# Eight-bank attention loops in a fused four-layer decoder: whole sequences per turn instead of half sequences

## The chip, the core and the metric

The kernel runs on one NeuronCore of a Trainium2 chip. The metric is the device time of one execution in microseconds (us), as a median of several runs; lower is better. The engines that matter are TensorE (PE in the profile; PEld are its weight loads), VectorE (DVE), ScalarE (ACT) and GpSimd (POOL). PSUM, into which TensorE writes, has eight banks of 128 partitions by 512 fp32 values.

## What is computed

Twelve layers run one after the other on x of shape (8, 128, 128): eight sequences of 128 tokens with 128 features. Five of them are 16-head attentions with head size 8 (three self-attentions, L1a, L3a and, with keys and values from ctx, L0x, all causal; L1x with a distance bias; L2x with an integer mask). Each comes down to this (scaling, mask and projections differ):

```python
scores = jnp.einsum('bhqd,bhkd->bhqk', query, key_) * scale
scores = jnp.where(causal, scores, -jnp.inf)
probs = jax.nn.softmax(scores, axis=-1)
attn = jnp.einsum('bhqk,bhkd->bhqd', probs, value)
attn = attn.transpose(0, 2, 1, 3).reshape(Bq, Sq, D)
return attn @ Wo.T
```

So one sequence has 16 score matrices of 128x128, or 128x2048 fp32 values, which fill four PSUM banks. The other layers (gated experts, a linear attention, a router) are not touched by the change.

## The kernel before

All instructions are written by hand, engine by engine, with semaphores. The eight sequences are two groups (g = 0, 1) of four (GB = 4). Each engine has one program for each group; the programs are generators that yield a pair (layer, phase), and `weave` always continues the one with the smallest pair. So the order on an engine is fixed when the kernel is built, by the phases; inside an attention loop they come from `beat`.

One attention of one group is done in eight units (UNITS = 8), u = 2b + half: a unit is half of the heads (eight) of sequence b. Two row strips of 32 partitions hold these heads: strip r holds the four heads 4r to 4r+3, and `KTm` holds the keys spread so that a 32-row matmul gives four heads' scores in one bank. The steps of a unit, in the names that the text uses:

- **M** (`masked`, `biased`, PE): the mask or bias is written to the unit's two banks by bf16 matmuls with the identity; one per bank, three per bank in L1x.
- **S** (`scores`, PE): one 32-row fp32 matmul of 512 columns per strip is added to it, in a bank of its own. An fp32 matmul is two MATMUL records in the profile.
- **R** and **sub** (DVE, L1258 and L1264): the row maximum of each head over the unit's 1024 columns, then the scores minus the maximum, to SBUF (`pr`).
- **T** (`turned`, PE, L458): eight transposes back to the same two banks.
- **exp** (ACT, L892): the exponential of the two banks to SBUF (`PT`).
- **W** (`weighted`, PE): eight matmuls with 32 output columns each, the values with a column of ones, to the bank `VALUES[g]`.
- **OT** (`weighted_out`, ACT, L860): after both halves the 128x512 result is copied to SBUF.

After the last unit, **back** (PE, L477) transposes the four copies, DVE divides by the sum that the column of ones gave (`normal`, `normal_last`, L1231 to L1241), and `out_proj` and a residual add end the layer.

Banks 0 and 7 are `VALUES`. The other six are three pairs, which the units of both groups take in turn (`pair(g, u)` is `PAIRS[(2u + g) % 3]`), so M of a unit waits for the exp of an earlier unit of the other group. POOL (L347) spreads the keys of each sequence into one of two halves of `KTm`.

Of the kernel before, what the change touches and what calls it, by code (L numbers as in the profile page):

```python
# [11 lines left out]
ACT = mybir.ActivationFunctionType  # L12
AX = mybir.AxisListType

P = 128
# [76 lines left out]
def build(nc, x_d, ctx_d, mask_d, w_d, r_d, c_d, k_d, b_d, out_d, marks):  # L92
# [165 lines left out]
    def beat(g, u, k=0):  # L258

        return 20 + 10 * u + 6 * g + k  # L260
# [49 lines left out]
    def _(pool):  # L310
# [13 lines left out]
        def program(g):  # L324
# [7 lines left out]
            def spread_keys(n, l):  # L332

                first = 0 if l in ("L1x", "L2x") else 1
                for b in range(first, GB):
                    yield n, ((1 + b if first == 0 else 19) if b < 2 else beat(g, 2 * b - 4, 3))
                    if b == first:
                        pool.wait_ge(*s.at(f"{l}.KT"))
                        if l == "L0x":
                            for other in range(GROUPS):  # L340
                                pool.wait_ge(*s.at("L0x.qrot", other))
                        if first == 0:
                            for other in range(GROUPS):
                                pool.wait_ge(*s.at(f"{l}.xn", other))
                    if b >= 2:
                        pool.wait_ge(*s.at(f"{l}.S{2 * b - 3}"))
# [46 lines left out]
    def _(pe):  # L393
        def mm(out, lhsT, rhs, start=True, stop=True, **k):
            return pe.matmul(out, lhsT, rhs, start=start, stop=stop, **k)  # L395
# [5 lines left out]
        def program(g):  # L401
# [22 lines left out]
            def attend(n, l):  # L424

                def biased(u, i):

                    r, out = 2 * (u % 2) + i, pair(g, u)[:, i, :]
                    if l == "L1x":
                        odd = out.rearrange("p (j k) -> p j k", j=HG)[:, 1::2, :]  # L430
                        mm(out, identb, alibi0[:, HG * r:HG * r + HG, :], stop=False)
                        mm(odd, identb, alibi1[:, 2 * r:2 * r + 2, :], start=False, stop=False)
                        mm(odd, identb, alibi2[:, 2 * r:2 * r + 2, :], start=False, stop=False)
                    else:
                        mask = t.dmask[:, u // 2, :] if l == "L2x" else causalb
                        mm(out, identb, mask.unsqueeze(1).to_broadcast([P, HG, P]), stop=False)

                def masked(u):
                    if 2 * u + g >= 3:
                        pe.wait_ge(*s.at(f"{l}.exp{(2 * u + g - 3) // 2}", 1 - g))  # L440
                    elif u:
                        pe.wait_ge(*s.at(f"{l}.QT", 1))
                    for i in range(2):
                        biased(u, i)

                def scores(u):
                    b, half = divmod(u, 2)
                    if half == 0:
                        pe.wait_ge(*s.at(f"{l}.keys{b}"))
                    for i in range(2):  # L450
                        r = 32 * (2 * half + i)
                        ins = mm(pair(g, u)[:, i, :], QT[r:r + 32, b * P:(b + 1) * P], t.KTm[r:r + 32, b % 2, :, :], start=False, tile_position=(r, 0))
                    ins.then_inc(*s.step(f"S{u}"))

                def turned(u):
                    pe.wait_ge(*s.at(f"{l}.sub{u}"))
                    for j in range(HH):
                        ins = pe.transpose(heads_of(pair(g, u))[:, j // HG, j % HG, :], pr[:, (u % 2) * HH + j, :], ident)  # L458
                    ins.then_inc(*s.step(f"T{u}"))

                def weighted(u):

                    b, half = divmod(u, 2)
                    if half == 0 and b:
                        pe.wait_ge(*s.at(f"{l}.OT{b - 1}"))
                    pe.wait_ge(*s.at(f"{l}.exp{u}"))
                    for j in range(HH):
                        h, at = HH * half + j, 32 * (j % HG)
                        ins = mm(VALUES[g][at:at + 32, h // HG * P:(h // HG + 1) * P], t.vaug[:, b, h, :], PT[:, (u % 2) * HH + j, :], tile_position=(0, at))
                    ins.then_inc(*s.step(f"O{u}"))  # L470

                def back(b):

                    pe.wait_ge(*s.at(f"{l}.OT{b}"))
                    for i in range(GB):
                        out = (VALUES[g] if b == GB - 1 else EARLIER[g][:, b, :])[:, i * P:(i + 1) * P]
                        ins = pe.transpose(out, t.ot[b][:, i * P:(i + 1) * P], ident)  # L477
                    ins.then_inc(*s.step(f"OR{b}"))

                pe.wait_ge(*s.at(f"{l}.KT"))  # L480
                pe.wait_ge(*s.at(f"{l}.vaug"))
# [22 lines left out]
                yield n, beat(g, UNITS, 1)  # L504
                if g == 0:
                    pe.wait_ge(*s.at(f"{l}.exp{UNITS - 1}", 1))
                for b in range(GB - 1):
                    back(b)
                yield n, beat(g, UNITS, 2)
                back(GB - 1)  # L510
# [336 lines left out]
    def _(act):  # L847
# [5 lines left out]
        def program(g):  # L853
# [31 lines left out]
            def attend(n, l):  # L885
                for u in range(UNITS):
                    yield n, beat(g, u, 4)
# [3 lines left out]
                    half = PT[:, (u % 2) * HH:(u % 2 + 1) * HH, :].rearrange("p (i j) k -> p i j k", i=2)  # L891
                    act.activation(half, heads_of(pair(g, u)), ACT.Exp, scale=SCALES[l]).then_inc(*s.step(f"exp{u}"))  # L892
                    if u >= 2 and u % 2 == 0:
                        yield n, beat(g, u, 5)
                        weighted_out(u // 2 - 1, l)
                yield n, beat(g, UNITS, 1)
                weighted_out(GB - 1, l)
                yield n, 130
                read(t.coT[:, :], bank(3 * g), "coTp", "coT")

            def weighted_out(b, l):
                read(t.ot[b], VALUES[g], f"O{2 * b + 1}", f"OT{b}")

# [189 lines left out]
    def _(dve):  # L1093
# [50 lines left out]
        def program(g):  # L1144
# [82 lines left out]
            def attend(n, l):  # L1227
                def normal():
                    dve.wait_ge(*s.at(f"{l}.OR{GB - 2}"))
                    O = EARLIER[g].rearrange("p b (h d) -> p b h d", h=H)  # L1230
# [5 lines left out]
                def normal_last():  # L1236
                    dve.wait_ge(*s.at(f"{l}.OR{GB - 1}"))
                    O = VALUES[g].rearrange("p (h d) -> p h d", h=H)
# [14 lines left out]
                for u in range(UNITS):  # L1253
                    yield n, beat(g, u, 1)
                    half = u % 2
                    S, top = heads_of(pair(g, u)), t.mx[:, half, :].rearrange("p (i j) -> p i j", i=2)
                    dve.wait_ge(*s.at(f"{l}.S{u}"))
                    dve.tensor_reduce(top, S, AX.X, ALU.max).then_inc(*s.step())  # L1258
                    reduced = s.last()
                    yield n, beat(g, u, 2)  # L1260
                    if u >= 2:
                        dve.wait_ge(*s.at(f"{l}.T{u - 2}"))
                    dve.wait_ge(*reduced)
                    dve.tensor_tensor(pr[:, half * HH:(half + 1) * HH, :].rearrange("p (i j) k -> p i j k", i=2), S,  # L1264
                                      top.unsqueeze(3).to_broadcast([P, 2, HG, P]), ALU.subtract).then_inc(*s.step(f"sub{u}"))
                yield n, beat(g, UNITS, 2)
                normal()
                yield n, beat(g, UNITS, 3)
# [507 lines left out]
```

## Time and profile before

| what | us |
|---|---|
| median of 3 runs | 725.29 |
| lowest and highest | 724.2, 726.57 |
| the profiled execution's own time | 725.43 |
| span of its instructions | 723.6 |
| PE busy | 591.4 (82%) |
| DVE busy | 471.8 (65%) |
| ACT busy | 255.7 (35%) |
| POOL busy | 98.6 (14%) |

The span runs from the first to the last instruction on the core; the 1.8 us between it and the run's own time lie around it. A busy share is a mean over all twelve layers, which have different limits, so the attention loops are read by themselves. PE counts a matmul until its modelled end, and the next may start before that: starts of successive instructions tell more than their durations.

### The profile page before, as it was taken

How to read it: one execution, taken by the hardware profiler on the slowest of the kernel's cores; microseconds unless marked ns; L12 is line 12 of the kernel's file. 1: busy time of each engine (PE TensorE's matmuls, PEld its weight loads, DVE VectorE, ACT ScalarE, POOL GpSimd, SP SyncE). 2: the span in 40 equal slices, each digit the busy share in tenths (PEclk: the TensorE clock that was granted, in tenths of full speed). 3: DMA queues.
4: the chain of work that ended last, by engine and by line, in shares of the span. 5: the costliest groups of instructions: out<-in, count | busy, mean ns of one | idle time of the engine just before them, and what ended most of it. 6: DMA issues, size and time to landing. Idle time of an engine off the chain costs nothing.

```text
span 723.6 us, 10686 instructions
## 1 busy us (share of the span) xinstructions
PE 591.4 (82%) x4265; PEld 389.8 (54%) x4265; DVE 471.8 (65%) x1200; ACT 255.7 (35%) x380; POOL 98.6 (14%) x101
## 2 busy tenths in 40 slices
PE   1425699976999889988997788999779978998477
PEld 1324355676455645565776755556435574556435
DVE  7687777577587566755247726775553468866685
ACT  2356334414344333333432442434221114443261
POOL 5021120014210041001002004200200012102120
PEclk9967589979899999997998999999789989999769
DMA  9700000000000000000000000000000000000000
GB/s 293 327 0 2 0 1 2 1 1 1 0 2 1 1 1 1 2 1 1 0 1 1 1 0 1 1 2 1 0 1 0 1 1 0 2 1 1 0 1 29
DMA packets 6720, 12.40 MB, mean 17 GB/s; under 512 B 528, under 2 KB 4880, under 8 KB 6288
## 3 DMA queue, kind: packets, MB, share of 16 engines
q1 hardware_dynamic: 6672, 11.73, 4.5%
q8 instruction: 33, 0.54, 0.3%
q14 instruction: 15, 0.12, 0.1%
HBM read 11.21 MB, written 0.52 MB: 16 GB/s over the span
## 4 chain that ended last, share of the span: by engine, by line
PE 69%; DVE 23%; ACT 3%; POOL 3%; issue 2%; DVEq 0%; ACTq 0%; POOLq 0%
PE ps L395 52%; PE ps L458 11%; DVE st L1151 3%; PE ps L411 3%; PE ps L477 2%; DVE xn L1347 2%; DVE mx L1258 2%; DVE big L1264 2%; POOL rs L330 2%; DVE mv L1154 1%; DVE x L1277 1%; PE ps L580 1%; ACT big L892 1%; DVE big L1190 1%; DVE ve L1156 1%
## 5 line engine op out<-in xcount | busy, mean ns | idle before, releaser
L1258 DVE TENSOR_REDUCE mx<-ps 128x8 f32<-128x1024 f32 x80 | 97.9, 1224 | 53.1 <-PE ps L395 52.9
L892 ACT ACTIVATE big<-ps 128x1024 f32<-128x1024 f32 x80 | 81.9, 1023 | 125.5 <-PE ps L458 125.5
L1264 DVE TENSOR_TENSOR big<-ps,mx 128x1024 f32<-128x1024 f32 x80 | 98.0, 1225 | 7.3 <-DVE mx L1258 0.5
L458 PE MATMUL ps<-kt,big 128*128 128x128 f32 x640 | 90.1, 285 | 8.1 <-DVE big L1264 7.9
L395 PE MATMUL ps<-KTm,qk 32*128 32x512 f32 x320 | 92.7, 658 | 0.0
L458 PEld LDWEIGHTS ps<-kt,big 128*128 128x128 f32 x640 | 70.7, 144 | 34.6 <-DVE big L1264 19.7
L330 POOL TENSOR_TENSOR rs<-ve,negh 128x4 f32<-128x4 f32 x26 | 26.5, 1021 | 406.3 <-DVE ve L1156 406.2
L395 PE MATMUL ps<-xnT,wt 128*128 128x512 f32 (+1 forms) x140 | 73.8, 667 | 3.1 <-DVE big L1539 3.1
L395 PEld LDWEIGHTS ps<-wt,big 128*128 128x128 f32 (+1 forms) x480 | 56.0, 191 | 10.9 <-issue 8.6
L395 PE MATMUL ps<-wt,big 128*128 128x128 f32 (+1 forms) x480 | 60.2, 280 | 1.1 <-ACT big L1041 1.1
L395 PEld LDWEIGHTS ps<-big,vaug 128*32 128x32 f32 x1280 | 30.4, 109 | 48.0 <-ACT big L892 45.5
L347 POOL TENSOR_TENSOR KTm<-qk,kt 128x512 f32<-128x512 f32 x34 | 37.4, 1107 | 127.9 <-PE ps L395 88.0
L411 PE MATMUL ps<-kt,xn 128*128 128x128 f32 x80 | 18.8, 378 | 39.3 <-DVE xn L1347 39.0
L395 PE MATMUL ps<-big,vaug 128*32 128x128 f32 x1280 | 50.5, 278 | 0.0
L395 PE MATMUL ps<-bt 128*128 128x512 bf16 (+1 forms) x192 | 46.8, 354 | 0.0
L860 ACT ACTIVATE xnT<-ps 128x512 f32<-128x512 f32 x30 | 17.9, 597 | 75.8 <-PE ps L411 65.5
L395 PEld LDWEIGHTS ps<-xnT,wt 128*128 128x128 f32 (+1 forms) x140 | 27.6, 212 | 31.6 <-issue 26.0
L395 PEld LDWEIGHTS ps<-KTm,qk 32*128 32x128 f32 x320 | 24.8, 189 | 33.9 <-issue 31.3
L1323 DVE SCALAR_TENSOR_TENSOR x<-ps,gw,x 128x128 f32<-128x128 f32 x80 | 22.2, 344 | 30.3 <-PE ps L395 29.5
L395 PEld LDWEIGHTS ps<-wt,xnT 128*128 128x128 f32 x256 | 38.1, 237 | 3.4 <-DVE big L1495 1.7
L395 PE MATMUL ps<-wt,xnT 128*128 128x128 f32 (+2 forms) x256 | 38.4, 313 | 1.5 <-DVE big L1495 1.5
L411 PEld LDWEIGHTS ps<-kt,xn 128*128 128x128 f32 x80 | 12.0, 187 | 44.4 <-issue 25.9
(274 smaller groups left out, 773.4 us busy)
## 6 DMA issues: line engine op xcount, KB each, us to landing
wt<-in_weights SPq DMA_DIRECT2D x1, 1664.0 KB, 17.3
wt<-in_weights SPq DMA_DIRECT2D x1, 1603.0 KB, 12.3
wt<-in_weights SPq DMA_DIRECT2D x6, 256.0 KB, 11.3
bt<-in_bconsts SPq DMA_DIRECT2D x1, 1024.0 KB, 8.7
rowt<-in_rows SPq DMA_DIRECT2D x1, 975.0 KB, 5.7
wt<-in_weights SPq DMA_DIRECT2D x1, 832.0 KB, 13.8
wt<-in_weights SPq DMA_DIRECT2D x1, 608.0 KB, 18.5
wt<-in_weights SPq DMA_DIRECT2D x1, 580.0 KB, 5.5
```

What stands on the lines that cost most here:

```text
L330: pool.tensor_tensor(out, src, negh[:, :], ALU.pow).then_inc(*s.step(name + "_r"))
L347: pool.tensor_tensor(t.KTm[:, b % 2, :, :], keys_of(t, b), own_head(), ALU.mult).then_inc(*s.step(f"keys{b}"))
L395: return pe.matmul(out, lhsT, rhs, start=start, stop=stop, **k)
L411: ins = pe.transpose(seq(bk, b), src[:, b, :], ident)
L458: ins = pe.transpose(heads_of(pair(g, u))[:, j // HG, j % HG, :], pr[:, (u % 2) * HH + j, :], ident)
L477: ins = pe.transpose(out, t.ot[b][:, i * P:(i + 1) * P], ident)
L860: act.activation(out, src, ACT.Copy).then_inc(*s.step(name))
L892: act.activation(half, heads_of(pair(g, u)), ACT.Exp, scale=SCALES[l]).then_inc(*s.step(f"exp{u}"))
L1151: dve.bn_stats(t.st[:, b, :], src[:, b, :]).then_inc(*s.step())
L1258: dve.tensor_reduce(top, S, AX.X, ALU.max).then_inc(*s.step())
L1264: dve.tensor_tensor(pr[:, half * HH:(half + 1) * HH, :].rearrange("p (i j) k -> p i j k", i=2), S, top.unsqueeze(3).to_broadcast([P, 2, HG ...
L1323: dve.scalar_tensor_tensor(x[:, b, :], bank(banks[e])[:, b * P:(b + 1) * P], gw[:, b, e:e + 1], x[:, b, :], ALU.mult, ALU.add).then_inc(*s ...
```

## The change

The two groups no longer share banks. Group g has banks 4g to 4g+3, and all four hold the scores of one whole sequence: strip r in bank r.

- M is written for four banks and S runs all four strips in a row, once for each sequence, with one semaphore step; `scores(b)` was two calls of two strips.
- R, sub, T, exp and W stay as they were in size and number (eight heads each). They work on `pair(g, half)`, banks 0 and 1 or 2 and 3 of the group.
- W of half 0 goes to bank 0 and W of half 1 to bank 2, each to 256 columns, after the exp of that half has read them. Each is copied by an own OT of 128x256. The masks of the next sequence follow bank by bank: bank 1 and bank 3 after the W, bank 0 and bank 2 after their OT.
- `back` writes sequence b to bank (b+1) % 4 of the group, in the order 0, 2, 1, 3.
- The phases (`beat`) count turns: turn 2b + g is sequence b of group g.

```diff
-    PAIRS = (all_banks[:, 1:3, :], all_banks[:, 5:7, :], all_banks[:, 3:5, :])
-    EARLIER = (all_banks[:, 1:4, :], all_banks[:, 4:7, :])
-    VALUES = tuple(all_banks[:, k, :] for k in (0, 7))
-
-    def pair(g, u):
-
-        return PAIRS[(2 * u + g) % 3]
+    def pair(g, half):
+
+        return all_banks[:, 4 * g + 2 * half:4 * g + 2 * half + 2, :]
...
-                def scores(u):
-                    b, half = divmod(u, 2)
-                    if half == 0:
-                        pe.wait_ge(*s.at(f"{l}.keys{b}"))
-                    for i in range(2):
-                        r = 32 * (2 * half + i)
-                        ins = mm(pair(g, u)[:, i, :], QT[r:r + 32, b * P:(b + 1) * P], t.KTm[r:r + 32, b % 2, :, :], start=False, tile_position=(r, 0))
-                    ins.then_inc(*s.step(f"S{u}"))
+                def scores(b):
+                    pe.wait_ge(*s.at(f"{l}.keys{b}"))
+                    for i in range(GB):
+                        r = 32 * i
+                        ins = mm(bank(i), QT[r:r + 32, b * P:(b + 1) * P], t.KTm[r:r + 32, b % 2, :, :], start=False, tile_position=(r, 0))
+                    ins.then_inc(*s.step(f"S{b}"))
...
-                masked(0)
+                masked(0, 1)
+                pe.wait_ge(*s.at(f"{l}.vaug"))
+                masked(0, 2)
                 if l in ("L1x", "L2x"):
                     yield n, 4
                     pe.wait_ge(*s.at(f"{l}.xnT"))
                     project_cols(0, xnT, w(f"{l}_wq"), "q")
+                masked(0, 3)
                 yield n, 20
                 pe.wait_ge(*s.at(f"{l}.QT"))
+                masked(0, 0)
                 scores(0)
-                for u in range(UNITS):
-                    yield n, beat(g, u, 2)
-                    turned(u)
-                    if u + 1 < UNITS:
-                        masked(u + 1)
-                        scores(u + 1)
-                    if u:
-                        weighted(u - 1)
-                yield n, beat(g, UNITS)
-                weighted(UNITS - 1)
...
+                for b in range(GB):
+                    turn, more = 2 * b + g, b + 1 < GB
+                    yield n, beat(turn - 1, 5)
+                    turned(2 * b)
+                    yield n, beat(turn, 0)
+                    turned(2 * b + 1)
+                    weighted(2 * b)
+                    if more:
+                        masked(b + 1, 1)
+                    weighted(2 * b + 1)
+                    if more:
+                        masked(b + 1, 3)
+                        pe.wait_ge(*s.at(f"{l}.OT{2 * b}"))
+                        masked(b + 1, 0)
+                        yield n, beat(turn, 6)
+                        pe.wait_ge(*s.at(f"{l}.OT{2 * b + 1}"))
+                        masked(b + 1, 2)
+                        scores(b + 1)
```

On PE, in the middle of the loop of L0x, the rows before are these, for one unit of each group (kt,big is T, bt is M, KTm,qk is S, big,vaug is W; the digit is the group; L395 and L391 are the helper that issues every matmul):

```order
L458 MATMUL ps<-kt,big0 128x128 x8
L395 MATMUL ps<-bt 128x512 x2
L395 MATMUL ps<-KTm0,qk0 128x512 x2
L395 MATMUL ps<-big0,vaug0 32x128 x8
L458 MATMUL ps<-kt,big1 128x128 x8
L395 MATMUL ps<-bt 128x512 x2
L395 MATMUL ps<-KTm1,qk1 128x512 x2
L395 MATMUL ps<-big1,vaug1 32x128 x8
```

And now, for one turn (one sequence of group 0) from its second T to its S:

```order
L444 MATMUL ps<-kt,big0 128x128 x8
L391 MATMUL ps<-big0,vaug0 32x128 x8
L391 MATMUL ps<-bt 128x512
L391 MATMUL ps<-big0,vaug0 32x128 x8
L391 MATMUL ps<-bt 128x512 x2
L444 MATMUL ps<-kt,big1 128x128 x8
L391 MATMUL ps<-bt 128x512
L391 MATMUL ps<-KTm0,qk0 128x512 x4
```

The W of a unit stood behind the S of the next one; now both W of a sequence stand between its second T and its next S, with the masks in between and the first T of the other group before the last mask.

On ACT, in the same place, before (L892 is exp, L860 is OT):

```order
L892 ACTIVATE big0<-ps 128x1024
L860 ACTIVATE td0<-ps 128x512
L892 ACTIVATE big1<-ps 128x1024
L860 ACTIVATE td1<-ps 128x512
L892 ACTIVATE big0<-ps 128x1024
```

And now:

```order
L884 ACTIVATE big0<-ps 128x1024 x2
L853 ACTIVATE td0<-ps 128x256 x2
L884 ACTIVATE big1<-ps 128x1024 x2
L853 ACTIVATE td1<-ps 128x256 x2
L884 ACTIVATE big0<-ps 128x1024 x2
```

The copies come right behind the second exp of their own sequence, where one copy for each sequence stood behind the first exp of the next.

## Rows read from the trace of the kernel before

**Rows 1.** The page, part 1: busy time, share and instructions of each engine.

```profile
PE 591.4 (82%) x4265; PEld 389.8 (54%) x4265; DVE 471.8 (65%) x1200; ACT 255.7 (35%) x380; POOL 98.6 (14%) x101
```

**Rows 2.** The page, part 5, the S matmuls: count | busy us, mean ns.

```profile
L395 PE MATMUL ps<-KTm,qk 32*128 32x512 f32 x320 | 92.7, 658 | 0.0
```

**Rows 3.** Windows from first R to last sub, per loop: engines' busy us, PEclk.

```profile
83.71:134.48 50.77, 50.34 (x418) 26.80 (x417) 39.20 (x32) 18.88 (x21) 4.16 (x4) 0.89 0.00 1
...
191.99:238.85 46.86, 45.35 (x418) 24.52 (x416) 39.10 (x32) 18.89 (x21) 4.16 (x4) 1.00 0.00 1
260.36:313.18 52.82, 50.66 (x472) 29.69 (x468) 39.10 (x32) 18.89 (x21) 5.04 (x5) 1.00 0.00 1
447.57:495.73 48.16, 45.92 (x416) 25.06 (x412) 39.10 (x32) 18.89 (x21) 5.75 (x6) 0.96 0.00 1
602.00:648.85 46.85, 45.35 (x418) 24.52 (x416) 39.10 (x32) 19.29 (x22) 4.88 (x5) 1.00 0.00 1
```

**Rows 4.** Timeline in the loop of L0x: start, us, engine, line, tiles, count.

```profile
107.23 1.22 DVE L1258 TENSOR_REDUCE mx<-ps 128x8 f32<-128x1024 f32 x1 [0.53 <-PE ps L395]
...
107.69 1.09 PE L458 MATMUL ps<-kt,big 128*128 128x128 f32 x8
...
108.56 1.23 DVE L1264 TENSOR_TENSOR big<-ps,mx 128x1024 f32<-128x1024 f32 x1
108.61 0.60 PE L395 MATMUL ps<-bt 128*128 128x512 bf16 x2
108.81 1.02 ACT L892 ACTIVATE big<-ps 128x1024 f32<-128x1024 f32 x1 [0.40 <-PE ps L458]
...
109.14 1.13 PE L395 MATMUL ps<-KTm,qk 32*128 32x512 f32 x4
...
110.20 0.64 PE L395 MATMUL ps<-big,vaug 128*32 128x128 f32 x16
110.31 1.23 DVE L1258 TENSOR_REDUCE mx<-ps 128x8 f32<-128x1024 f32 x1 [0.53 <-PE ps L395]
...
110.77 1.09 PE L458 MATMUL ps<-kt,big 128*128 128x128 f32 x8
```

**Rows 5.** Timeline at the end of the loop of L0x.

```profile
134.53 1.09 PE L458 MATMUL ps<-kt,big 128*128 128x128 f32 x8 [0.49 <-DVE big L1264]
...
135.55 1.08 PE L395 MATMUL ps<-big,vaug 128*32 128x128 f32 x32
135.66 1.02 ACT L892 ACTIVATE big<-ps 128x1024 f32<-128x1024 f32 x1 [1.13 <-PE ps L458]
...
136.74 0.66 PE L477 MATMUL ps<-kt,td 128*128 128x128 f32 x4
```

**Rows 6.** Timeline at the starts of the loops of L1a and L1x.

```profile
190.29 0.59 PE L395 MATMUL ps<-bt 128*128 128x512 bf16 x2
...
190.81 0.30 PEld L395 LDWEIGHTS ps<-KTm,qk 32*128 32x128 f32 x4 [0.42 <-issue]
...
257.38 1.88 PE L395 MATMUL ps<-xnT,wt 128*128 128x512 f32 x4
...
259.19 1.99 PE L395 MATMUL ps<-KTm,qk 32*128 32x512 f32 x8
...
263.83 1.03 PE L395 MATMUL ps<-bt 128*128 128x512 bf16 x6
```

**Rows 7.** Windows as in Rows 3, at the starts of L0x and L2x.

```profile
74.00:94.50 20.50, 15.89 (x46) 7.48 (x48) 13.66 (x16) 5.54 (x8) 3.92 (x3) 0.50 0.00 0
...
449.50:452.90 3.40, 2.79 (x12) 1.89 (x12) 2.91 (x3) 0.79 (x1) 0.00 (x0) 0.50 0.00 0
```

**Rows 8.** Timeline in these stretches: T in L2x, M and S in L0x.

```profile
450.11 1.97 PE L458 MATMUL ps<-kt,big 128*128 128x128 f32 x8 [1.73 <-DVE big L1264]
...
80.60 1.06 PE L395 MATMUL ps<-bt 128*128 128x512 bf16 x2
...
81.59 2.08 PE L395 MATMUL ps<-KTm,qk 32*128 32x512 f32 x4
```

More of the change, by code:

```diff
@@ L256, in last, with beat @@
             return semaphores[self.sem], self.count[self.sem] - back
-    def beat(g, u, k=0):
-        return 20 + 10 * u + 6 * g + k
+    def beat(turn, k=0):
+        return 30 + 10 * turn + k
     SCALES = {l: float(P if l == "L2x" else HD) ** -0.5 for l in ("L0x", "L1a", "L1x", "L2x", "L3a")}
@@ L335, in spread_keys @@
                 for b in range(first, GB):
-                    yield n, ((1 + b if first == 0 else 19) if b < 2 else beat(g, 2 * b - 4, 3))
+                    yield n, ((1 + b if first == 0 else 19) if b < 2 else beat(2 * (b - 2) + g))
                     if b == first:
@@ L345, in spread_keys @@
                     if b >= 2:
-                        pool.wait_ge(*s.at(f"{l}.S{2 * b - 3}"))
+                        pool.wait_ge(*s.at(f"{l}.S{b - 2}"))
                     pool.tensor_tensor(t.KTm[:, b % 2, :, :], keys_of(t, b), own_head(), ALU.mult).then_inc(*s.step(f"keys{b}"))
@@ L424, in attend, with masked @@
             def attend(n, l):
-                def biased(u, i):
-                    r, out = 2 * (u % 2) + i, pair(g, u)[:, i, :]
+                def masked(b, r):
+                    out = bank(r)
                     if l == "L1x":
@@ L434, in biased @@
                     else:
-                        mask = t.dmask[:, u // 2, :] if l == "L2x" else causalb
+                        mask = t.dmask[:, b, :] if l == "L2x" else causalb
                         mm(out, identb, mask.unsqueeze(1).to_broadcast([P, HG, P]), stop=False)
[L438 to L442, printed above, removed]
-                    for i in range(2):
-                        biased(u, i)
-                def scores(u):
-                    b, half = divmod(u, 2)
-                    if half == 0:
-                        pe.wait_ge(*s.at(f"{l}.keys{b}"))
-                    for i in range(2):
-                        r = 32 * (2 * half + i)
-                        ins = mm(pair(g, u)[:, i, :], QT[r:r + 32, b * P:(b + 1) * P], t.KTm[r:r + 32, b % 2, :, :], start=False, tile_position=(r, 0))
-                    ins.then_inc(*s.step(f"S{u}"))
+                def scores(b):
[4 more added lines that the diff above has]
+                    ins.then_inc(*s.step(f"S{b}"))
                 def turned(u):
@@ L457, in turned @@
                     for j in range(HH):
[L458 removed]
+                        ins = pe.transpose(heads_of(pair(g, u % 2))[:, j // HG, j % HG, :], pr[:, (u % 2) * HH + j, :], ident)
                     ins.then_inc(*s.step(f"T{u}"))
@@ L463, in weighted @@
                     b, half = divmod(u, 2)
-                    if half == 0 and b:
-                        pe.wait_ge(*s.at(f"{l}.OT{b - 1}"))
                     pe.wait_ge(*s.at(f"{l}.exp{u}"))
                     for j in range(HH):
-                        h, at = HH * half + j, 32 * (j % HG)
-                        ins = mm(VALUES[g][at:at + 32, h // HG * P:(h // HG + 1) * P], t.vaug[:, b, h, :], PT[:, (u % 2) * HH + j, :], tile_position=(0, at))
+                        at = 32 * (j % HG)
+                        ins = mm(bank(2 * half)[at:at + 32, j // HG * P:(j // HG + 1) * P], t.vaug[:, b, HH * half + j, :], PT[:, half * HH + j, :],
+                                 tile_position=(0, at))
                     ins.then_inc(*s.step(f"O{u}"))
                 def back(b):
-                    pe.wait_ge(*s.at(f"{l}.OT{b}"))
                     for i in range(GB):
-                        out = (VALUES[g] if b == GB - 1 else EARLIER[g][:, b, :])[:, i * P:(i + 1) * P]
-                        ins = pe.transpose(out, t.ot[b][:, i * P:(i + 1) * P], ident)
+                        ins = pe.transpose(seq((b + 1) % GB, i), t.ot[b][:, i * P:(i + 1) * P], ident)
                     ins.then_inc(*s.step(f"OR{b}"))
                 pe.wait_ge(*s.at(f"{l}.KT"))
-                pe.wait_ge(*s.at(f"{l}.vaug"))
                 if l == "L1x":
@@ L490, in attend @@
                     project_cols(0, xnT, w(f"{l}_wq"), "q")
+                masked(0, 3)
                 yield n, 20
                 pe.wait_ge(*s.at(f"{l}.QT"))
+                masked(0, 0)
                 scores(0)
-                for u in range(UNITS):
-                    yield n, beat(g, u, 2)
-                    turned(u)
-                    if u + 1 < UNITS:
-                        masked(u + 1)
-                        scores(u + 1)
-                    if u:
-                        weighted(u - 1)
-                yield n, beat(g, UNITS)
-                weighted(UNITS - 1)
[L504 to L509, printed above, removed]
+                for b in range(GB):
[16 more added lines that the diff above has]
+                        scores(b + 1)
+                yield n, beat(2 * GB + g)
+                back(0)
+                back(2)
+                pe.wait_ge(*s.at(f"{l}.OT{UNITS - 1}"))
+                back(1)
                 back(GB - 1)
@@ L885, in attend, with exponentials @@
             def attend(n, l):
-                for u in range(UNITS):
-                    yield n, beat(g, u, 4)
+                def exponentials(u):
+                    half = u % 2
                     act.wait_ge(*s.at(f"{l}.T{u}"))
@@ L890, in attend, with weighted_out @@
                         act.wait_ge(*s.at(f"{l}.O{u - 2}"))
[L891 to L897, printed above, removed]
+                    act.activation(PT[:, half * HH:(half + 1) * HH, :].rearrange("p (i j) k -> p i j k", i=2), heads_of(pair(g, half)),
+                                   ACT.Exp, scale=SCALES[l]).then_inc(*s.step(f"exp{u}"))
+                def weighted_out(u):
+                    b, half = divmod(u, 2)
+                    read(t.ot[b][:, 2 * half * P:2 * (half + 1) * P], bank(2 * half)[:, 0:2 * P], f"O{u}", f"OT{u}")
+                for b in range(GB):
+                    turn = 2 * b + g
+                    yield n, beat(turn - 1, 5)
+                    exponentials(2 * b)
+                    yield n, beat(turn, 0)
+                    exponentials(2 * b + 1)
+                    weighted_out(2 * b)
+                    weighted_out(2 * b + 1)
                 yield n, 130
                 read(t.coT[:, :], bank(3 * g), "coTp", "coT")
-            def weighted_out(b, l):
-                read(t.ot[b], VALUES[g], f"O{2 * b + 1}", f"OT{b}")
             for n, l in enumerate(LAYERS[1:STAGES + 1]):
@@ L1228, in normal @@
                 def normal():
-                    dve.wait_ge(*s.at(f"{l}.OR{GB - 2}"))
-                    O = EARLIER[g].rearrange("p b (h d) -> p b h d", h=H)
+                    dve.wait_ge(*s.at(f"{l}.OR1"))
+                    O = all_banks[:, 4 * g + 1:4 * g + GB, :].rearrange("p b (h d) -> p b h d", h=H)
                     dve.reciprocal(t.rc3[:, :, :], O[:, :, :, HD]).then_inc(*s.step())
@@ L1237, in normal_last @@
                     dve.wait_ge(*s.at(f"{l}.OR{GB - 1}"))
-                    O = VALUES[g].rearrange("p (h d) -> p h d", h=H)
+                    O = bank(0).rearrange("p (h d) -> p h d", h=H)
                     dve.reciprocal(t.rc[:, :], O[:, :, HD]).then_inc(*s.step())
@@ L1253, in attend @@
                 for u in range(UNITS):
[L1254 to L1257, printed above, removed]
+                    b, half = divmod(u, 2)
+                    yield n, beat(2 * b + g, 1 + half)
+                    S, top = heads_of(pair(g, half)), t.mx[:, half, :].rearrange("p (i j) -> p i j", i=2)
+                    dve.wait_ge(*s.at(f"{l}.S{b}"))
                     dve.tensor_reduce(top, S, AX.X, ALU.max).then_inc(*s.step())
-                    reduced = s.last()
-                    yield n, beat(g, u, 2)
                     if u >= 2:
                         dve.wait_ge(*s.at(f"{l}.T{u - 2}"))
-                    dve.wait_ge(*reduced)
+                    dve.wait_ge(*s.last())
                     dve.tensor_tensor(pr[:, half * HH:(half + 1) * HH, :].rearrange("p (i j) k -> p i j k", i=2), S,
                                       top.unsqueeze(3).to_broadcast([P, 2, HG, P]), ALU.subtract).then_inc(*s.step(f"sub{u}"))
-                yield n, beat(g, UNITS, 2)
+                yield n, beat(2 * GB + g, 2)
                 normal()
-                yield n, beat(g, UNITS, 3)
+                yield n, beat(2 * GB + g, 3)
                 normal_last()
```

## The prediction, before the changed kernel ran

> **What bounds the kernel now.** I read the page's busy shares first: PE 82%, DVE 65% [rows 1]. These are means over twelve layers, so next the windows of the five attention loops, cut from the first R to the last sub. In all of them PE is busy nearly throughout: 45.35 of 46.86 us in L1a, 50.66 of 52.82 in L1x, while DVE has 39.1 in each [rows 3]. Together the loops last 245.5 us, a third of the run, and nothing outside them is changed except their starts and ends. The timeline of one unit in L0x then gives the cycle [rows 4]. T starts at 107.69, M at 108.61, S at 109.14, W at 110.20, the next T at 110.77: T 0.92, M 0.53, S 1.06, W 0.57, in sum 3.08 us with no gap. R starts at 107.23 and again at 110.31, the same 3.08. DVE works 2.46 of it and waits 0.53 for PE. So PE sets the pace, at 6.17 us for the two units of a sequence.
>
> **What S costs, and why it can shrink.** Two strips take 1.06 us from start to start of what follows. The four S records of a unit have a mean of 658 ns (92.7 us of PE for 320 of them [rows 2]), yet four fit in 1.13 us [rows 4]: the two strips run side by side and the two passes of fp32 one behind the other. The W of a unit, sixteen records of four column strips, fit in 0.64 us [rows 4], so four strips of the other kind run side by side already. Four row strips, each with its own bank, don't stand in the trace. From below, nothing is added for strips 2 and 3 (S stays 1.06 for a whole sequence); from above, they run behind the first two (2.12). I take 1.06, because both W and the pairs of S show full overlap; the upper end is a rival below. By this PE has 1.06 less work for each sequence, 5.1 instead of 6.17.
>
> The Trainium skill weighs here (TensorE: Matmul & The Clock Gate, part 3, measured speedup against the span model): its model adds some 4 ns per strip, as I take it, but its table gives four row strips of 512 columns as 3.07 times one, not 4. The trace agrees with the model for two strips (four records in 1.13 us). The table is the second rival.
>
> **One turn, step by step** (start = second T of group 0's sequence; PE order as in the order of the changed kernel). T to W is 1.02 (134.53 to 135.55 [rows 5]), since the kind of matmul changes. First W 0.57, to 1.59. One M, about half of 0.53, to 1.9. The second W needs the second exp. That one starts 1.13 after its T starts, takes 1.02, and lets PE go on 2.21 after T (134.53, 135.66, 136.74 [rows 5]). So the second W starts at 2.21, and PE has stood for 0.3: a new wait, with W, three M, the other group's T and S queued behind it. W to 2.78, M of banks 3 and 0 to 3.31, T of the other group 0.92 to 4.23 (its sub ended long before, see below), M of bank 2 0.27 to 4.50, S 1.06 to 5.56. The two OT waits add nothing: a copy of 256 columns is bounded by 1.02 us, the 1024-column exp, and I estimate 0.4; the first starts at 2.15 behind the exp and is done by 2.6, before 3.05 when M of bank 0 comes; the second starts at 2.85 and is done by 3.3, before 4.23. ACT is busy some 2.9 of 5.55. POOL's spread of the keys waits for the S of two sequences before, which is done two turns earlier, and POOL is busy 4 to 6 us in a whole loop [rows 3]. **A turn takes 5.55 us against 6.17.**
>
> DVE per sequence: R to sub 1.33 (107.23 to 108.56), sub 1.23, twice, in sum 5.15 [rows 4]. That is under 5.55, so PE stays the bound by 0.4, and the gain of 1.06 on PE loses 0.3 to the exp wait and some 0.1 to changes of kind.
>
> **A whole loop is not 8 turns.** Before, the first units run faster than 3.08, as there is no W yet: 46.86 us in L1a, not 16 x 3.08 = 49.3. Now the start is DVE's: first R at 0, last sub of group 0 at 5.15, T at 5.20. Turns 0 to 5 each issue the S for two turns later, whose R starts 1.17 after S (109.14 to 110.31), 5.67 after the turn's start. The last sequence's R starts at 5.20 + 5 x 5.55 + 5.67 = 38.6, its last sub ends at **43.8 us**. In L1x a mask has three matmuls; six for two banks last about 1.0 us where two last 0.53 [rows 6, 4], so 0.22 more per bank; one is hidden under the exp wait, three are not: turn 6.2, loop 5.20 + 31.0 + 6.3 + 5.15 = 47.7.
>
> **Starts.** Group 0 now needs four banks masked before its first S. In L1a and L3a PE is the bound there (M at 190.29, S at 190.81, no gap [rows 6]): +0.5 each. In L2x and L1x M of bank 3 of both groups moves behind the projections and M of bank 0 behind QT: three masks between the projection and S, less the slack until QT is ready: about +0.65 in L2x, 3 x 0.48 = +1.4 in L1x (projections from 257.38, S at 259.19 [rows 6]). In L0x the clock is at half and two masks cost 1.06 of PE [rows 8]: +0.9.
>
> **Ends.** After the last sub: T, W, exp wait, W, now 16 `back` transposes of each group without a W between them, where one W stood between. By the same steps it comes out within 0.2 us of before: nothing.
>
> **Sum against the profiled execution's own time, 725.4** (0.1 above the median). L1a and L3a: 46.86 to 43.8, less 0.5, saves 2.5 each. L2x: 48.16 to 43.8, less 0.65, saves 3.7. L1x: 52.82 to 47.7, less 1.4, saves 3.7. L0x starts at half clock until 94.5 [rows 7]: first R at 84.6, T of turn 0 only at 90.2, W, M and W at half speed, S at 96.4, then 5.55 a turn: last sub at 130.5 against 134.48, saves 4.0. Total 16.4, which gives 709.0.
>
> **The clock takes some back.** The granted clock was 0.50, that is 1.2 of 2.4 GHz, from 449.50 to 452.90, at the start of L2x's loop [rows 7]; PE had just stood for 1.73 us waiting for the first sub, and T took 1.97 instead of 1.09 [rows 8]. Now PE stands longer at every start: in the first 5.2 us it has S of group 1 and a single T, some 2 us of waiting. I assume that in three of the four starts that were at full clock the clock falls once for some 3.4 us, at 1 us each: T is 0.9 longer and partly on the path. That is +3 us. **Forecast 712.0 us, 13.4 less.** It could be 0 (709) or, with longer falls, +8 (717).
>
> **Rivals.**
> 1. *Four strips overlap only in part.* By 4/3.07 a set of four would take 1.30 times one strip's time, S 1.38 instead of 1.06: +0.32 in six places of each of five loops and in the first S, 35 times, +11 us: 723. For it: writing four banks at once is new. Against it: two row strips and four column strips show no loss at all. The factor is the table's of the skill page named above; any loss of 0.3 would give the same.
> 2. *The strips don't overlap by more than two.* S is 2.12, a turn 6.6, a plain loop 50.0 (5.20 + 33.0 + 6.7 + 5.15), the first S 1.06 later: L1a and L3a +4.7 each, L2x and L1x about +3.5 each, L0x +4, in sum +20: **745, slower**. It decides from an S of about 1.5 on, where 35 times the excess is the 16.4 us saved above. Then the exp wait, the later starts and the lost fast first units are paid without a gain.
> 3. *DVE is the bound.* If the changes of kind cost less and the exp wait closes, a turn falls to DVE's 5.15: 0.4 x 6 x 5 = 12 us less; that needs PE to find work for the wait, which its order doesn't allow. Half of it is thinkable: 705.
> 4. *Nothing changes*, since starts and the clock eat it all: each loop would have to lose 3.3 us more than above. The clock would have to be at half for most of turn 0 and 1 in all loops: about 722 to 727.
>
> **Chances.** Forecast with its clock term between 0 and +6 (708 to 716): 0.58. Rival 3 or part of it: 0.12. Rival 1 or more clock loss (716 to 723): 0.17. Rival 4: 0.06. Rival 2 or another slower case: 0.07. The range 704 to 722 leaves out about 0.17. A measurement tells about 0.3% from no change (2.2 us): faster 0.89, same 0.04, slower 0.07.
>
> **What the profile after would show.** The eight S records of a sequence within about 1.15 us, their starts in two sets of four (rival 2: four sets of two, 2.2 us; rival 1: records longer than 692 ns). R of successive sequences every 5.55 us, with DVE idle about 0.4 before the first R and none before the second. PE idle about 0.3 before the second W, released by exp. Loops near 44 us, 48 in L1x. PE's busy time lower by some 40 us, DVE's and POOL's unchanged, ACT's up by some 7 (40 more copies, half as long). A granted clock of 0.5 in the first 10 us of loops that had 1.0. I would be wrong if S is longer with four banks written at once, if PE waits for an OT, or if the first turns lose more than 1 us each to the clock.

## The result

The changed kernel takes **699.59 us** (median of 4 runs, 699.31 to 701.01); before, 724.75 (median of 4 runs, 723.8 to 726.57). The ratio is 0.9654, 95% interval 0.963 to 0.9678. That is 25 us less, where 13.4 were forecast, and below the range of 704 to 722. The direction and the overlap of four strips came as predicted; what the prediction said of the clock did not, and the forecast of 712.0 is 12.4 us above the median.

The page after, parts 1 and 5, stands against [rows 1, 2]:

```profile
PE 546.0 (78%) x4265; PEld 374.0 (54%) x4265; DVE 467.8 (67%) x1200; ACT 258.2 (37%) x420; POOL 98.6 (14%) x101
...
L391 PE MATMUL ps<-KTm,qk 32*128 32x512 f32 x320 | 46.5, 652 | 0.0
```

PE is busy 45 us less, and the 320 S records account for all of it: 92.7 to 46.5 us at the same mean of one (658 and 652 ns). They overlap by four where they overlapped by two.

The windows of the five loops after (first R to last sub, columns as in [rows 3]), then of the stretch behind L3a's loop, after and before:

```profile
84.79:127.76 42.97, 37.96 (x428) 22.62 (x426) 38.35 (x32) 19.96 (x29) 4.17 (x4) 1.00 0.00 1
185.74:228.72 42.98, 37.98 (x428) 22.62 (x426) 38.35 (x32) 19.96 (x29) 4.17 (x4) 1.00 0.01 1
251.27:298.52 47.25, 42.84 (x475) 26.56 (x473) 38.34 (x32) 19.96 (x29) 4.17 (x4) 1.00 0.01 1
433.18:476.15 42.97, 37.32 (x425) 22.44 (x424) 38.34 (x32) 19.96 (x29) 5.23 (x6) 1.00 0.00 1
582.32:625.30 42.98, 37.98 (x428) 22.64 (x426) 38.35 (x32) 19.96 (x29) 4.38 (x5) 1.00 0.01 1
625.30:697.50 72.20, 51.00 (x302) 35.21 (x302) 46.64 (x218) 24.54 (x43) 10.48 (x10) 0.89 0.03 8
...
648.85:723.60 74.75, 53.99 (x318) 37.50 (x318) 46.65 (x218) 25.13 (x44) 10.48 (x10) 0.86 0.03 8
```

All four plain loops take the same time, with the clock at full speed in all of them. L0x gains 7.8 us, L1a and L3a 3.9, L1x 5.6, L2x 5.2: 26.3 in sum. Of this some 5 us are clock: before, L0x's loop is 3.9 and L2x's 1.3 us longer than L1a's, each with a stretch at a granted 0.50 at its start [rows 3, 7], and now all are equal. The starts give back some 2.8; the stretch behind the last loop, whose work nobody changed, is 2.6 shorter here.

One turn of L0x after (timeline; T is L444, S has KTm,qk, W has big,vaug, M has bt):

```profile
100.68 1.09 PE L444 MATMUL ps<-kt,big 128*128 128x128 f32 x8
100.82 1.22 DVE L1256 TENSOR_REDUCE mx<-ps 128x8 f32<-128x1024 f32 x1 [0.47 <-PE ps L391]
...
101.70 0.64 PE L391 MATMUL ps<-big,vaug 128*32 128x128 f32 x16
...
102.28 0.39 PE L391 MATMUL ps<-bt 128*128 128x512 bf16 x1
...
102.89 0.64 PE L391 MATMUL ps<-big,vaug 128*32 128x128 f32 x16 [0.22 <-ACT big L884]
103.28 1.21 DVE L1256 TENSOR_REDUCE mx<-ps 128x8 f32<-128x1024 f32 x1
103.46 0.61 PE L391 MATMUL ps<-bt 128*128 128x512 bf16 x2
...
103.91 1.04 PE L444 MATMUL ps<-kt,big 128*128 128x128 f32 x8
...
104.78 0.38 PE L391 MATMUL ps<-bt 128*128 128x512 bf16 x1
...
105.09 1.14 PE L391 MATMUL ps<-KTm,qk 32*128 32x512 f32 x8
106.16 1.09 PE L444 MATMUL ps<-kt,big 128*128 128x128 f32 x8
```

Eight S records fit in 1.14 us, where four took 1.13 [rows 4], and the next T follows 1.07 after S, where it was 1.06. A turn is 5.48 us (100.68 to 106.16). DVE waits 0.47 for PE before the first R of a sequence and not before the second; PE waits 0.22 for exp (L884) before the second W. The prediction had 5.55, 0.4 and 0.3.

### The profile page after: what moved, and what is told of

Its sections match the earlier page's. It is cut to its first block, busy times and chain, and to the rows that moved or that the text cites. A ratio compares the mean times of both kernels' runs of the same rounds, so it can differ in the third digit from the quotient of the medians.

```text
span 697.5 us, 10675 instructions
## 1 busy us (share of the span) xinstructions
PE 546.0 (78%) x4265; PEld 374.0 (54%) x4265; DVE 467.8 (67%) x1200; ACT 258.2 (37%) x420; POOL 98.6 (14%) x101
## 4 chain that ended last, share of the span: by engine, by line
PE 63%; DVE 23%; ACT 8%; POOL 2%; issue 2%; DMA 1%; SPq 0%; DVEq 0%; ACTq 0%
PE ps L391 46%; PE ps L444 10%; ACT big L884 5%; PE ps L407 3%; DVE st L1149 3%; DVE big L1260 3%; PE ps L460 2%; DVE mx L1256 2%; DVE xn L1343 2%; POOL rs L326 2%; DMA co<-in_ctx 1%; DVE mv L1152 1%; DVE x L1273 1%; PE ps L573 1%; DVE ve L1154 1%
## 5 line engine op out<-in xcount | busy, mean ns | idle before, releaser
L884 ACT ACTIVATE big<-ps 128x1024 f32<-128x1024 f32 x80 | 81.9, 1023 | 114.8 <-PE ps L444 114.8
L444 PE MATMUL ps<-kt,big 128*128 128x128 f32 x640 | 85.7, 277 | 17.3 <-DVE big L1260 17.3
L444 PEld LDWEIGHTS ps<-kt,big 128*128 128x128 f32 x640 | 70.7, 141 | 52.4 <-DVE big L1260 43.1
L391 PE MATMUL ps<-xnT,wt 128*128 128x512 f32 (+1 forms) x140 | 74.6, 670 | 3.1 <-DVE big L1535 3.1
L391 PEld LDWEIGHTS ps<-wt,big 128*128 128x128 f32 (+1 forms) x480 | 56.0, 191 | 10.3 <-issue 8.6
L391 PE MATMUL ps<-wt,big 128*128 128x128 f32 (+1 forms) x480 | 60.1, 279 | 0.8 <-ACT big L1039 0.8
L391 PE MATMUL ps<-big,vaug 128*32 128x128 f32 x1280 | 51.5, 279 | 10.6 <-ACT big L884 10.6
L391 PE MATMUL ps<-bt 128*128 128x512 bf16 (+1 forms) x192 | 49.4, 352 | 0.0
L391 PE MATMUL ps<-KTm,qk 32*128 32x512 f32 x320 | 46.5, 652 | 0.0
L853 ACT ACTIVATE xnT<-ps 128x512 f32<-128x512 f32 (+1 forms) x40 | 19.6, 489 | 70.3 <-PE ps L407 65.5
L391 PEld LDWEIGHTS ps<-big,vaug 128*32 128x32 f32 x1280 | 30.1, 109 | 28.8 <-ACT big L884 22.1
L391 PEld LDWEIGHTS ps<-xnT,wt 128*128 128x128 f32 (+1 forms) x140 | 27.7, 214 | 31.1 <-issue 25.6
L391 PEld LDWEIGHTS ps<-wt,xnT 128*128 128x128 f32 x256 | 38.3, 238 | 3.4 <-DVE big L1491 1.7
L391 PE MATMUL ps<-wt,xnT 128*128 128x128 f32 (+2 forms) x256 | 38.4, 313 | 1.5 <-DVE big L1491 1.5
L1535 DVE TENSOR_TENSOR big<-ps,big 128x512 f32<-128x512 f32 (+1 forms) x18 | 12.3, 689 | 29.1 <-PE ps L391 29.1
```

The source lines that it names most:

```text
L444: ins = pe.transpose(heads_of(pair(g, u % 2))[:, j // HG, j % HG, :], pr[:, (u % 2) * HH + j, :], ident)
L853: act.activation(out, src, ACT.Copy).then_inc(*s.step(name))
L884: act.activation(PT[:, half * HH:(half + 1) * HH, :].rearrange("p (i j) k -> p i j k", i=2), heads_of(pair(g, half)), ACT.Exp, scale=SCALE ...
```

## Experiments: is the gain the overlap of four strips?

**s_pairs: the order undone that lets four strips stand in a row.** The mask of bank 2 moves between strips 1 and 2, from the second sequence of each group on; all instructions stay.

```diff
                     for i in range(GB):
                         r = 32 * i
+                        if b and i == 2:
+                            pe.wait_ge(*s.at(f"{l}.OT{2 * b - 1}"))
+                            masked(b, 2)
...
-                        pe.wait_ge(*s.at(f"{l}.OT{2 * b + 1}"))
-                        masked(b + 1, 2)
                         scores(b + 1)
```

> The changed kernel with one order undone: from the second sequence on, the mask of bank 2 stands between strips 0, 1 and strips 2, 3 of S, so that only two strips can run side by side; the instructions are the same. Theory 1 (the gain is that strips 2 and 3 cost nothing beside 0 and 1): S takes two times 1.06 and a turn goes from 5.48 to about 6.6; 5 loops x 6 turns x 1.1 = +33 us, 733 us, slower than before. Theory 2 (the gain comes from the new order and the own banks, S being of little weight): under +10 us, below 710.

Measured: 733.71 us, ratio to before 1.0118 (1.0093 to 1.0144), so 1.2% slower than before, a small difference that is clear of the noise. Its timeline in L1a:

```profile
208.43 1.13 PE L391 MATMUL ps<-KTm,qk 32*128 32x512 f32 x4
209.49 0.39 PE L391 MATMUL ps<-bt 128*128 128x512 bf16 x1
209.81 1.13 PE L391 MATMUL ps<-KTm,qk 32*128 32x512 f32 x4
210.87 1.09 PE L447 MATMUL ps<-kt,big 128*128 128x128 f32 x8
```

From S to the next T it is 2.44 us now (208.43 to 210.87), with the mask in it. Theory 1 expected 733. New order, own banks and split W by themselves make the kernel 9 us slower; the four strips side by side are worth 34 us, more than the whole gain. This is the prediction's second rival in all but the first S of each group, which keeps its four strips here. The rival had 745, 11 us more: about 5 (five times 1.06) for those first S, some 3 for L0x at half clock until 94.5 (here the clock is up at 84.6, as in the changed kernel), and 2.6 for the stretch behind the last loop. Its plain loop of 50.0 us measured 49.84.

**two_strips: strips 2 and 3 left out.**

```diff
-                    for i in range(GB):
+                    for i in range(2):
                         r = 32 * i
...
```

In banks 2 and 3 the mask matmuls' `start` and `stop` flags change with it, as no S is added there; their number and order stay.

> The changed kernel without the S of strips 2 and 3 (half of the scores is left out; everything else, masks, exponentials and W of all heads too, stays). Theory 1 (strips 2 and 3 run beside 0 and 1 and cost nothing): the turn stays at 5.48 to within 0.03, 699 to 700 us. Theory 2 (four banks written at once cost something, the skill table's 3.07 for 4): S falls by up to 0.3, up to 9 us faster.

Measured: 699.41 us, ratio 0.9641 (0.9583 to 0.97). Its timeline shows a turn of 5.47 us and four S records in 1.13:

```profile
100.46 1.13 PE L391 MATMUL ps<-KTm,qk 32*128 32x512 f32 x4
101.52 1.09 PE L444 MATMUL ps<-kt,big 128*128 128x128 f32 x8
...
105.93 1.13 PE L391 MATMUL ps<-KTm,qk 32*128 32x512 f32 x4
```

Two strips cost 1.06 us on PE and four 1.07. The prediction's first rival, an S of 1.38, is out. (This is the rival of the table; the sentence of the prediction that calls the table the second rival has the number wrong.) The two totals agree partly by chance, since in two_strips the clock was low in the first turns of L0x and L2x. Where it was at 1.00 in both kernels the loops can be compared: 42.85 us with two strips and 42.98 with four in L1a, 47.13 and 47.25 in L1x.

The Trainium skill (TensorE: Matmul & The Clock Gate, part 3, measured speedup against the span model) has a speedup of 3.07 for four row strips of 512 columns in its table, and some 4 ns for each further strip in its span model. By the table the prediction estimated 1.38 us. This trace is near the model and not the table: two further strips add 0.01 us.

## Experiments: what sets the turn now?

**exp_halves: the second exponential in two instructions.** The first half starts after four of the eight transposes.

```diff
+                        if u % 2 and j == HG - 1:
+                            ins.then_inc(*s.step(f"T{u}a"))
...
+                    if half:
+                        act.wait_ge(*s.at(f"{l}.T{u}a"))
+                        if u >= 2:
+                            act.wait_ge(*s.at(f"{l}.O{u - 2}"))
+                        for i in range(2):
+                            if i:
+                                act.wait_ge(*s.at(f"{l}.T{u}"))
+                            act.activation(PT[:, HH + i * HG:HH + (i + 1) * HG, :], heads_of(pair(g, 1))[:, i], ACT.Exp,
+                                           scale=SCALES[l]).then_inc(*s.step(f"exp{u}"))
+                        return
```

> The changed kernel with the second exponential of each sequence in two instructions of 512 columns, the first started after four of the eight transposes, so that the second W need not wait. Theory 1 (the wait of about 0.25 us for that exp is on the path, as PE sets the turn): a turn goes from 5.48 to about 5.25 in the plain loops, unchanged in L1x to within 0.05; 4 x 6 x 0.23 + ends = -5 to -6 us, 694 us. Theory 2 (DVE, which works 5.03 of 5.48, or the longer ACT time takes over): less than 2 us gained.

Measured: 693.05 us, ratio 0.9558 (0.9536 to 0.9581), 6.5 us less than the changed kernel. A turn of 5.19 us in its timeline:

```profile
100.37 1.09 PE L444 MATMUL ps<-kt,big 128*128 128x128 f32 x8
100.49 1.23 DVE L1268 TENSOR_REDUCE mx<-ps 128x8 f32<-128x1024 f32 x1 [0.18 <-PE ps L391]
...
102.29 0.64 PE L391 MATMUL ps<-big,vaug 128*32 128x128 f32 x16
...
105.56 1.09 PE L444 MATMUL ps<-kt,big 128*128 128x128 f32 x8
```

The second W starts 1.92 us after T instead of 2.21, and PE no longer stands before it. The exp wait that the change brought was on the path: 0.29 us of each plain turn. L1x gained a little too, against the expectation: its loop took 46.82 us instead of 47.25.

**grouped: besides, the mask of bank 1 before the first W**, so that both W stand together:

```diff
                     turned(2 * b + 1)
-                    weighted(2 * b)
                     if more:
+                        pe.wait_ge(*s.at(f"{l}.exp{2 * b}"))
                         masked(b + 1, 1)
+                    weighted(2 * b)
                     weighted(2 * b + 1)
```

> The kernel with the halved second exponential, and besides the mask of bank 1 moved from between the two W to before the first, so that both W stand together and PE changes its kind of matmul two times less in a turn. Theory 1 (a change of kind costs PE some 0.09 each and PE still sets the turn of 5.19): the turn goes to about 5.0, where DVE (4.91 busy and its gaps) takes over; 0.15 x 30 = -4 to -5 us against 693.05, 688.5 us. Theory 2 (a wait for the second half of the exp takes the place of what is saved, or DVE is the bound already): within 1 us of 693.

Measured: **685.79 us**, ratio 0.9449 (0.939 to 0.9507), the fastest kernel here and faster than both given ones. Its timeline:

```profile
99.88 1.09 PE L444 MATMUL ps<-kt,big 128*128 128x128 f32 x8
99.92 1.22 DVE L1269 TENSOR_REDUCE mx<-ps 128x8 f32<-128x1024 f32 x1
...
101.12 1.24 PE L391 MATMUL ps<-big,vaug 128*32 128x128 f32 x32
...
104.99 1.09 PE L444 MATMUL ps<-kt,big 128*128 128x128 f32 x8
105.12 1.23 DVE L1269 TENSOR_REDUCE mx<-ps 128x8 f32<-128x1024 f32 x1 [0.20 <-PE ps L391]
```

A turn is 5.11 (99.88 to 104.99) and the next one 5.2, where about 5.0 was expected, and DVE waits at every second sequence only. The median is 7.3 us below exp_halves, where 4 to 5 were expected. The loops of the two profiled executions hold 4.4 of it: L1x went from 46.82 to 45.35 us (bias matmuls stood between its two W), three plain loops from 41.26 to 40.90, and L2x from 42.75 to 40.90, as the clock had fallen in its start in exp_halves. Of the 1.9 us in L2x, 1.5 are therefore the clock's and not the edit's. The rest, some 3 us, lies outside the loops, in work that is the same in both, 2.1 of it behind the last loop (75.5 and 73.4 us); I put it down to the clock of the two executions, which wasn't separated. In L1x a turn went from 6.06 to 5.82 us, 0.12 for each change of kind that is gone. A plain turn gains less, as waits take the place of what is saved: the two W start 1.17 us before the next mask there (101.12 to 102.29) and 1.01 in L1x.

## Experiments: where does the clock come in?

The loop of L0x gained 7.8 us, twice as much as L1a's; 3.9 of it are clock. In before it starts at a granted clock of 0.50 until 94.5 us [rows 7]; in the changed kernel this ends at 84.6:

```profile
71.00:84.60 13.60, 6.90 (x24) 3.24 (x24) 8.85 (x15) 6.64 (x10) 2.88 (x2) 0.50 0.00 0
84.60:94.50 9.90, 7.80 (x80) 4.61 (x80) 9.52 (x8) 3.19 (x5) 2.08 (x2) 1.00 0.01 2
```

Is that the kernel or the execution? Both kernels were profiled again.

**b_again**, the kernel before:

> The kernel before, unchanged, profiled once more. Question: is its slow start of L0x's loop (granted clock 0.50 until 94.5 us, loop 50.77 us) and of L2x's loop (0.50 from 449.5 to 452.9, loop 48.16) a property of the kernel or of one execution? Theory A (property: the first units of before give TensorE too little work at these places): L0x's loop again 50 to 51 us, L2x's above 47.5. Theory B (chance of an execution): these two loops scatter, L0x's between 47 and 51, and other loops may be the slow ones. Both expect 723 to 727 us.

**a_again**, the changed kernel:

> The changed kernel, unchanged, profiled once more. Theory A: all four plain loops again 42.97 us and L1x 47.25, with the clock at 1.00 in all of them. Theory B: one or more loops show a stretch at 0.50 and are 1 to 3 us longer. The stretch after L3a's loop (72.20 us here, 74.75 in before) should be the same under A, and scatter by 1 to 3 us under B. Both expect 699 to 701 us.

726.51 and 701.29 us. Before: L0x's loop 50.91 us (clock low until 95.6), L2x's 48.16, L1a's 46.85: the same to 0.2 us. After: L0x's 42.95 (low until 87.3), but in L1a the clock fell once, for one stretch, and that loop took 44.21 instead of 42.98. Windows of L1a in a_again, loop and stretch:

```profile
188.11:232.32 44.21, 39.43 (x428) 23.57 (x426) 38.36 (x32) 20.09 (x29) 4.16 (x4) 0.96 0.01 1
...
193.10:196.50 3.40, 3.40 (x28) 2.22 (x28) 3.37 (x3) 1.41 (x2) 0.00 (x0) 0.50 0.00 0
```

So a fall of the clock in the first turns costs 1.2 us, near the prediction's 1 us, but it is rare: in the three profiled executions of the changed kernel (a third is below) the twelve starts other than L0x's show it once, where I had assumed three in four. Of the variants, exp_halves and two_strips show one each, in L2x, at 1.5 and 1.9 us. The stretch behind L3a's loop was 74.2 us, 2 longer than in the first profile, so its 2.6 us of gain can't be credited to the change. For the kernel before Theory A holds at both places: L2x's loop is 48.16 us in all three of its profiled executions (b_fourth is below), with the same stretch of 3.4 us at 0.50. For the changed kernel it holds in L0x's loop, and Theory B at the one fall in L1a and in the stretch behind L3a.

**first_pairs: only the first S of each group in two pairs.**

```diff
                     for i in range(GB):
                         r = 32 * i
+                        if b == 0 and i == 2:
+                            masked(0, 2)
...
-                masked(0, 2)
```

> The changed kernel with the first S of each group in two pairs, the mask of bank 2 between them; the later S as four strips. Looks at the granted clock at the start of L0x's loop, which left 0.50 at 84.6 and 87.3 us in two executions of the changed kernel and only at 94.5 and 95.6 in two of before. Theory A (four strips side by side in the first S are what brings the clock up): it stays at 0.50 into the nineties, and L0x's loop is 2 us or more longer than 43. Theory B (not S but the doubled masks or the moment decide): up by about 88, loop at 43 to 44. Both expect first R some 1 us later in each loop, about 5 us in all.

Measured: 706.96 us. The clock in L0x stayed low to 95.6 and its loop took 46.0 us; L1a's loop was 42.95, as in the changed kernel. Windows of first_pairs, to be held against those of the changed kernel above:

```profile
84.60:94.50 9.90, 9.90 (x25) 3.46 (x25) 6.22 (x6) 0.00 (x0) 2.08 (x2) 0.50 0.00 0
...
87.11:133.12 46.01, 42.89 (x428) 24.70 (x427) 38.43 (x32) 19.98 (x29) 4.16 (x4) 0.91 0.00 1
191.67:234.62 42.95, 39.07 (x428) 22.92 (x426) 38.33 (x32) 19.98 (x29) 4.16 (x4) 1.00 0.01 1
```

The total is 7.4 us above the changed kernel, 5 of it expected from the later starts. One execution could be chance, so first_pairs and both given kernels were profiled once more, as first_pairs_3, a_fourth and b_fourth.

> The kernel whose first S of each group is in two pairs, profiled a second time. So far the clock at the start of L0x's loop came up at 91.1 us or later in all four executions whose first S has two strips at a time (before twice, this kernel once, the one without strips 2 and 3 once) and by 87.3 in all five whose first S has four. Theory A (four strips at once bring it up): again after 90, L0x's loop 44 to 46 us. Theory B (chance of the execution): as likely by 88 with a loop near 43.

> The changed kernel, profiled once more. Theory A: the clock is up by 88 us and L0x's loop takes 42.97 us. Theory B: it may stay low into the nineties, with a loop of 44 to 46.

> The kernel before, profiled once more. Theory A: the clock stays low past 91 us, L0x's loop 48 to 51 us. Theory B: it may be up by 88, with a loop near 47.

Theory A three times: clock low until 98.1, 83.2 and 95.4; loops of L0x 46.81, 42.95 and 50.85 us (712.24, 697.98 and 723.86 us in all). The same window in a_fourth, b_fourth and first_pairs_3:

```profile
83.20:95.40 12.20, 10.12 (x104) 5.75 (x104) 10.68 (x9) 3.90 (x6) 3.12 (x3) 1.00 0.00 1
...
83.20:95.40 12.20, 12.20 (x36) 5.35 (x34) 7.35 (x6) 2.05 (x2) 1.61 (x2) 0.50 0.00 0
...
83.20:95.40 12.20, 12.20 (x32) 4.39 (x29) 7.04 (x6) 0.38 (x1) 2.44 (x3) 0.50 0.00 0
```

Counted over all runs: with two strips at a time in the first S the clock came up at 91.1 or later in six of six executions (before three times, first_pairs twice, two_strips once), with four at a time by 87.3 in six of six (the changed kernel three times, s_pairs, exp_halves, grouped). That the first S decides rests on two kernels: first_pairs differs from the changed kernel in the pairs of the first S and the place of one mask, and two_strips leaves all masks where they are and halves S (its later S too, and it ran in one profiled execution). So neither the doubled masks nor the place of that mask alone explains it. PE had no gap while the clock stayed low: 9.90 of 9.90 us in first_pairs, 12.20 of 12.20 in b_fourth. Why it stays low with two strips at a time is not settled: the runs show only that the same S records, side by side by four, go with an early rise in every execution.

## Why the prediction was wrong in size

Held against its own steps, from 712.0 down to the profiled 699.3:

| step | predicted | measured | adds |
|---|---|---|---|
| clock falls at the other loops' starts | +3 | 0 in this execution | 3.0 |
| L0x at half clock until 94.5, as before | loop 45.9, of which 43.8 at full clock | full clock | 2.1 |
| length of a loop at full clock, five loops | 43.8, 47.7 | 42.97, 47.25 | 3.8 |
| starts of the loops | +4.0 | +2.8 | 1.2 |
| stretch behind the last loop | 0 | -2.6 | 2.6 |

- **The clock was the step that failed**, with 5.1 of the 12.7 us. "The clock takes some back" had the price about right and the number of falls wrong: three in four starts assumed, none in this execution, one in twelve over three. It argued from PE's waiting. PE did wait 1.86 of the first 5.20 us of L1a's loop, near the 2 us predicted, and the clock stayed at 1.00, while the PE of L0x's start, busy without a gap, stayed at 0.50 in before. I had carried before's clock in L0x over as if it were given; it went with the two-strip S that the change removes. The 2.6 us behind the last loop are scatter that no step could have forecast: that stretch took 72.2 to 74.8 us over the executions of both kernels.
- **The loop's length** was the other term that was too large, with 3.8 us: the first sequence takes DVE 4.88 us to the end of its last sub (the next R starts at 4.79), not 5.15, since its sub has no wait for a T (R to sub 1.26 us instead of 1.33); the last takes 5.03; and the turn is 5.48, not 5.55. Three small sums on the high side, 0.8 us in each plain loop. Rows on DVE in L1a of the changed kernel:

```profile
185.74 1.23 DVE L1256 TENSOR_REDUCE mx<-ps 128x8 f32<-128x1024 f32 x1 [1.53 <-PE ps L391]
187.00 1.22 DVE L1260 TENSOR_TENSOR big<-ps,mx 128x1024 f32<-128x1024 f32 x1
188.15 1.21 DVE L1256 TENSOR_REDUCE mx<-ps 128x8 f32<-128x1024 f32 x1
...
190.53 1.22 DVE L1256 TENSOR_REDUCE mx<-ps 128x8 f32<-128x1024 f32 x1
```

- **Right**: that PE was the bound and stays it; that strips 2 and 3 cost nothing; the new wait for the second exp and its size; the two OT waits without effect; the start of L1a (+0.5); L1x's turn (predicted 6.2, measured 6.13). PE's busy time fell by 45 us (40 predicted), ACT's rose by only 2.5 (7 predicted) and DVE's fell by 4.0 (none predicted). None of these three sets the pace of a turn.
- **Right by number only would be rival 3**: in full it takes 12 us from 712, which gives 700. But its mechanism didn't come: the turn is 5.48 us and not DVE's 5.15, and DVE still waits 0.47 for PE in it.
- **Starts**: L0x +1.1, L1a +0.5, L1x +1.0, L2x +0.3 and L3a -0.1, predicted 0.9, 0.5, 1.4, 0.65 and 0.5. L0x's number is not shown to be the change's: its first R came at 83.7, 84.5 and 84.4 us in the three executions of before and at 84.8, 86.3 and 83.7 in those of the changed kernel. L3a's may be the clock ahead of it; not tested.
- **The range** was too narrow below: its low end had room for a faster turn, none for clock gained. Its upper half held only losses that the rows of before did not show.

## What to carry to other kernels

Where heads are short and a matmul uses only 32 rows, issue all four row strips in a row, each into its own bank: here strips 2 and 3 cost 0.01 us, and one mask between the pairs cost 34 us of 700. When such a change shortens the bound, look for the wait that its new order makes (here the second exp) and split the work that is waited for: two small edits took the ratio to before from 0.965 to 0.945. And don't carry the clock of the old trace over to the new kernel: profile twice, and compare loops whose clock is the same.

## What the runs showed that I had not expected

- PE busy without a gap stayed at half clock: 9.90 of 9.90 us at a granted 0.50 with the 32-row matmuls of the first S in pairs. With four strips at once the clock was up by 87.3 us in every execution.
- A change of the kind of matmul costs: two fewer in a turn, with the mask moved, took 1.5 us off L1x's loop and 0.36 off a plain one, where DVE has nearly become the bound and the second W waits for exp again.
- Whole loops repeat to 0.03 us between executions where the clock is the same (42.95 to 42.98 in eleven plain loops of the changed kernel); what scatters between runs of one kernel is where the clock falls.
